# Two self attentions of a perceiver block: turned outputs in the sums' bank, the weighing one step later, projections over four banks

## The reference, cut to what matters

```python
def _L0_attn_ref(x, w_qkv, b_qkv, w_out, b_out):
    qkv = x @ w_qkv + b_qkv
    q, k, v = split into 16 heads of 16          # 4 batches of 256 rows
    attn = softmax(q @ k^T / 4)
    return heads(attn @ v) @ w_out + b_out
def _L1_attn_ref(x, W_qkv, W_proj, b_proj, lambda_q1, ..., subln_w):
    q, k: 32 heads of 8, v: 16 heads of 16       # 4 batches of 256 rows
    o = softmax(q1 @ k1^T) @ v - lam * softmax(q2 @ k2^T) @ v
    o = o * rsqrt(mean(o * o) + EPS) * subln_w * (1 - LAMBDA_INIT)
    return heads(o) @ W_proj + b_proj
```

## Time and profile before

| | us |
|---|---|
| median of 3 executions | 4051.34 (4047.96 to 4053.66) |
| the profiled execution, its own time | 4062.04 |
| its span, first to last instruction | 4059.9 |
| busy in it: PE / DVE / ACT / POOL | 3569.0 / 2493.9 / 2291.5 / 1661.4 |
| first self attention's core | from 1984.1 to 2117.2 |
| second self attention's core | from 3556.5 to 3749.3 |

### The profile page before, as it was taken

The page is one execution under the profiler, slowest core; times in us unless marked ns, Lnnn a source line. Parts: engine busy times, 40 slices in busy tenths (PEclk is TensorE's granted clock), DMA queues, the critical chain, the costliest instruction groups (busy, mean ns, idle before and its releaser), DMA issues. The chain is left out here.

```text
span 4059.9 us, 81431 instructions
## 1 busy us (share of the span) xinstructions
PE 3569.0 (88%) x30262; PEld 2602.5 (64%) x30262; DVE 2493.9 (61%) x3852; ACT 2291.5 (56%) x4294; POOL 1661.4 (41%) x1365
## 2 busy tenths in 40 slices
PE   6899999999999999997777976799999887677399
PEld 4678778777888878885446974455555443333298
DVE  6666666666666666663364113687878777367587
ACT  3666676666766666665242112466666666345165
POOL 1677777777777777767032002101010000024033
PEclk9999999999999999999888987799999999789599
DMA  6677766777767766661303656888878654000011
GB/s 244 250 293 285 273 253 259 278 275 275 260 258 278 272 253 229 246 242 57 86 7 130 256 193 234 184 167 180 168 180 167 128 70 57 15 11 1 21 48 42
DMA packets 231719, 723.30 MB, mean 178 GB/s; under 512 B 47372, under 2 KB 128524, under 8 KB 162444
## 3 DMA queue, kind: packets, MB, share of 16 engines
q1 hardware_dynamic: 228640, 709.70, 55.2%
q0 software_dynamic: 2688, 8.39, 0.6%
HBM read 623.61 MB, written 94.37 MB: 177 GB/s over the span
## 5 line engine op out<-in xcount | busy, mean ns | idle before, releaser
L784 POOL TENSOR_TENSOR wa_acc<-wa_acc,wa_probs 128x512 f32<-128x512 f32 x960 | 1258.2, 1311 | 459.4 <-ACT wa_probs L629 343.2
L694 DVE TENSOR_REDUCE wa_mx<-wa_ps_x 128x1 f32<-128x512 f32 x1024 | 658.6, 685 | 361.2 <-PE wa_ps_x L482 361.2
L629 ACT ACTIVATE wa_probs<-wa_ps_s 128x512 f32<-128x512 f32 x1024 | 531.3, 604 | 547.3 <-PE wa_ps_s L525 546.8
L1326 DVE TENSOR_REDUCE na_mx<-na_ps_m 128x2 f32<-128x1024 f32 x512 | 614.0, 1220 | 208.6 <-PE na_ps_m L1147 204.9
L1271 ACT ACTIVATE na_probs<-na_ps_s 128x512 f32<-128x512 f32 x1024 | 556.5, 595 | 324.1 <-PE na_ps_s L1167 321.7
L621 ACT ACTIVATE wa_ps_s<-wa_m_wide 128x512 f32<-128x512 f32 x1024 | 579.6, 616 | 0.0
L503 PE MATMUL wa_ps_o<-wa_probs,wa_values 128*64 128x256 f32 x4096 | 468.7, 381 | 0.0
L447 PE MATMUL wa_ps_x<-wa_k_ctx,wa_w_k 128*128 128x512 f32 x1488 | 381.0, 403 | 7.4 <-DMA wa_k_ctx<-ctx_split 6.7
L503 PEld LDWEIGHTS wa_ps_o<-wa_probs,wa_values 128*64 128x64 f32 x4096 | 285.4, 137 | 158.4 <-ACT wa_probs L629 23.8
L470 PE MATMUL wa_ps_x<-wa_w_v,wa_v_ctx 128*128 128x256 f32 x2880 | 364.6, 284 | 0.1
L470 PEld LDWEIGHTS wa_ps_x<-wa_w_v,wa_v_ctx 128*128 128x128 f32 x2880 | 357.7, 192 | 6.4 <-issue 0.5
(11 more groups left out here) (347 smaller groups left out, 5735.5 us busy)
## 6 DMA issues: line engine op xcount, KB each, us to landing
wa_k_ctx<-ctx_split SPq DMA_DIRECT2D x248, 1024.0 KB, 7.0
wa_v_ctx<-ctx_split SPq DMA_DIRECT2D x120, 1024.0 KB, 8.2
na_ctx<-ctx_split SPq DMA_DIRECT2D x56, 1024.0 KB, 11.6
na_keys<-k_rows SPq DMA_DIRECT2D x384, 128.0 KB
ctx_split<-wa_stage SPq DMA_DIRECT2D x32, 1024.0 KB, 5.0
w_land<-in_ctxT SPq DMA_DIRECT2D x32, 512.0 KB, 11.1
ge_w_b<-in_w_rows SPq DMA_DIRECT2D x8, 2048.0 KB, 7.8
k_rows<-na_k_high SPq DMA_DIRECT2D x64, 256.0 KB, 3.0
```

Source lines behind the costliest of these rows:

```text
L629: act.activation(probs[:, c % R:c % R + 2, h * SQ:(h + 1) * SQ], ps_s[n % BANKS][:, :].rearrange("p (c n) -> p c n", c=2), ACT.Exp).then_i ...
L694: dve.tensor_reduce(mx[:, half, h, k:k + 1], ps_x[banks[h]][:, :], AX.X, ALU.max).then_inc(m_taken, 1)
L784: pool.tensor_tensor(to[:, :], to[:, :], probs[:, c % R, :], ALU.add).then_inc(summed, 1)
L1326: dve.tensor_reduce(mx[:, half, :, k], ps_m[n % 2][:, :, :], AX.X, ALU.max).then_inc(m_taken, 1)
```

## The change

Four edits, all in self_attention:

1. The turned outputs go into the upper half of ps_o, beside the sums (columns 256 to 511), except those of the last step but one, which stay in ps_q. turn_shift no longer waits for `taken`; weigh does, since it writes the bank that VectorE reads.
2. In TensorE's loop the weighing is that of step n-2 instead of n-1, and stands before scores(n, 0), which itself moves behind turn_shift and maximum.
3. Values and query/key pieces rotate over four banks each instead of two; the values start when their own two DMAs have landed (`wv_in`).
4. VectorE clears ps_o after the first split_maximum instead of before the first maximum; only weigh(0) waits for it.

```diff
+        value_banks = [ps_q, ps_o, ps_m[1][:, 0, :], ps_m[1][:, 1, :]]
+        column_banks = [*ps_s, ps_m[0][:, 0, :], ps_m[0][:, 1, :]]
...
+        def turned(n):
+            return ps_q[:, 0:SQ] if n == STEPS - 2 else ps_o[:, SQ:2 * SQ]
...
-                sp.dma_start(w_sb[:, k, 2 * D:3 * D], w[k * P:(k + 1) * P, 2 * D:3 * D]).then_inc(w_in, 16)
+                sp.dma_start(w_sb[:, k, 2 * D:3 * D], w[k * P:(k + 1) * P, 2 * D:3 * D]).then_inc(wv_in, 16)
...
-                if t >= 2:
-                    pe.wait_ge(v_ready, t - 1)
+                if t >= 4:
+                    pe.wait_ge(v_ready, t - 3)
...
-                if n >= 2:
-                    pe.wait_ge(high_ready, n - 1)
-                    pe.wait_ge(low_ready, n - 1)
+                if n >= 4:
+                    pe.wait_ge(high_ready, n - 3)
+                    pe.wait_ge(low_ready, n - 3)
...
             def turn_shift(n):
                 pe.wait_ge(msplit_ready, n + 1)
-                if n >= 5:
-                    pe.wait_ge(taken, n - 4)
-                elif n:
+                if n:
                     pe.wait_ge(q_ready, n)
...
             def weigh(n):
                 pe.wait_ge(exp_done, 4 * n + 4)
                 if n:
                     pe.wait_ge(ov_ready, n)
+                if 0 < n < STEPS - 1:
+                    pe.wait_ge(taken, n)
+                elif n:
+                    pe.wait_ge(taken, n - 1)
+                else:
+                    pe.wait_ge(zeroed, 1)
...
             def turn_back(n):
                 pe.wait_ge(ov_ready, n + 1)
-                pe.wait_ge(q_ready, min(n + 5, STEPS))
-                if n >= STEPS - 4:
-                    pe.wait_ge(taken, n)
+                if n == STEPS - 2:
+                    pe.wait_ge(q_ready, STEPS)
...
-            pe.wait_ge(w_in, 16 * 2 * KD)
+            pe.wait_ge(wv_in, 16 * KD)
             for t in range(NT):
                 project_values(t)
+            pe.wait_ge(w_in, 16 * KD)
...
-            pe.wait_ge(zeroed, 1)
...
             for n in range(STEPS):
-                scores(n, 0)
+                if n == 0:
+                    scores(n, 0)
                 if n + 2 < STEPS:
                     turn_shift(n + 2)
                 if n + 3 < STEPS:
                     maximum(n + 3, 0)
                     maximum(n + 3, 1)
                 if n >= 2:
+                    weigh(n - 2)
+                if n:
+                    scores(n, 0)
+                if n >= 2:
                     turn_back(n - 2)
                 scores(n, 1)
-                if n:
-                    weigh(n - 1)
+            weigh(STEPS - 2)
             turn_back(STEPS - 2)
...
-            dve.memset(ps_o[:, :], 0.0).then_inc(zeroed, 1)
             for n in range(3):
                 take_maximum(n, 0)
                 if n:
                     shift(n - 1)
                 take_maximum(n, 1)
                 split_maximum(n)
+                if n == 0:
+                    dve.memset(ps_o[:, :], 0.0).then_inc(zeroed, 1)
```

More of the change, by code:

```diff
@@ L1501, in self_attention @@
         ps_q, ps_o = ps_two[1][:, 0, :], ps_two[1][:, 1, :]
-        turned = ps_q[:, 0:SQ].rearrange("p (a i d) -> p a i d", a=2, i=4)
-        w_in, const_in, bias_in = s.sem("w_in"), s.sem("const_in"), s.sem("bias_in")
+        value_banks = [ps_q, ps_o, ps_m[1][:, 0, :], ps_m[1][:, 1, :]]
+        column_banks = [*ps_s, ps_m[0][:, 0, :], ps_m[0][:, 1, :]]
+        wv_in, w_in, const_in, bias_in = s.sem("wv_in"), s.sem("w_in"), s.sem("const_in"), s.sem("bias_in")
         fixed, zeroed = s.sem("fixed"), s.sem("zeroed")
@@ L1580, in project @@
                 th, ct = divmod(n, 4)
-                if n >= 2:
-                    pe.wait_ge(high_ready, n - 1)
-                    pe.wait_ge(low_ready, n - 1)
+                if n >= 4:
+                    pe.wait_ge(high_ready, n - 3)
+                    pe.wait_ge(low_ready, n - 3)
                 for k in range(KD):
-                    ins = pe.matmul(ps_s[n % 2][:, :], w_sb[:, k, ct * P:(ct + 1) * P], xT[:, k, th * 512:(th + 1) * 512],
+                    ins = pe.matmul(column_banks[n % 4], w_sb[:, k, ct * P:(ct + 1) * P], xT[:, k, th * 512:(th + 1) * 512],
                                     start=(k == 0), stop=(k == KD - 1))
@@ L1662, in turn_back @@
                 pe.wait_ge(ov_ready, n + 1)
-                pe.wait_ge(q_ready, min(n + 5, STEPS))
-                if n >= STEPS - 4:
-                    pe.wait_ge(taken, n)
+                if n == STEPS - 2:
+                    pe.wait_ge(q_ready, STEPS)
                 for half in range(2):
-                    ins = pe.transpose(ps_q[:, half * P:(half + 1) * P], ov[n % 2][:, half * P:(half + 1) * P], ident[:, :])
+                    ins = pe.transpose(turned(n)[:, half * P:(half + 1) * P], ov[n % 2][:, half * P:(half + 1) * P], ident[:, :])
                 ins.then_inc(a_done, 1)
-            pe.wait_ge(w_in, 16 * 2 * KD)
+            pe.wait_ge(wv_in, 16 * KD)
             for t in range(NT):
                 project_values(t)
+            pe.wait_ge(w_in, 16 * KD)
             for n in range(8):
@@ L1709, in take_high @@
                 if bias is None:
-                    act.activation(high[:, n, :], ps_s[n % 2][:, :], ACT.Copy).then_inc(high_ready, 1)
+                    act.activation(high[:, n, :], column_banks[n % 4], ACT.Copy).then_inc(high_ready, 1)
                 else:
-                    act.activation(high[:, n, :], ps_s[n % 2][:, :], ACT.Identity, bias=bias_cols[:, n % 4:n % 4 + 1]
+                    act.activation(high[:, n, :], column_banks[n % 4], ACT.Identity, bias=bias_cols[:, n % 4:n % 4 + 1]
                                    ).then_inc(high_ready, 1)
@@ L1756, in take_values @@
                 dve.wait_ge(v_done, t + 1)
-                bank = (ps_o if t % 2 else ps_q)[:, 0:D]
+                bank = value_banks[t % 4][:, 0:D]
                 if diff:
@@ L1809, in take_out @@
             def take_out(n):
+                back = turned(n).rearrange("p (a i d) -> p a i d", a=2, i=4)
                 dve.wait_ge(a_done, n + 1)
@@ L1812, in take_out @@
                     dve.wait_ge(taken, n)
-                link(dve.reciprocal(rden[:, :, :], turned[:, :, :, DV]))
+                link(dve.reciprocal(rden[:, :, :], back[:, :, :, DV]))
                 if not diff:
@@ L1817, in take_out @@
                     for j in range(2):
-                        ins = dve.tensor_tensor(to[:, :, :, (h + j) * DV:(h + j + 1) * DV], turned[:, :, 2 * j:2 * j + 2, 0:DV],
+                        ins = dve.tensor_tensor(to[:, :, :, (h + j) * DV:(h + j + 1) * DV], back[:, :, 2 * j:2 * j + 2, 0:DV],
                                                 rden[:, :, 2 * j:2 * j + 2].unsqueeze(3).to_broadcast([P, 2, 2, DV]), ALU.mult)
@@ L1825, in take_out @@
                     to = o_rows[:, 2 * b:2 * b + 2, 4 * g * DV:4 * (g + 1) * DV].rearrange("p a (i d) -> p a i d", i=4)
-                    dve.tensor_tensor(to, turned[:, :, :, 0:DV], wide, ALU.mult).then_inc(taken, 1)
+                    dve.tensor_tensor(to, back[:, :, :, 0:DV], wide, ALU.mult).then_inc(taken, 1)
                     return
@@ L1830, in take_out @@
                     dve.wait_ge(joined, n // 2 - 1)
-                dve.tensor_tensor(second[n // 2 % 2][:, :, :, :], turned[:, :, :, 0:DV], wide, ALU.mult).then_inc(taken, 1)
+                dve.tensor_tensor(second[n // 2 % 2][:, :, :, :], back[:, :, :, 0:DV], wide, ALU.mult).then_inc(taken, 1)
             dve.wait_ge(fixed, 3)
```

6 lines of the change are left out of this document (3 added, 3 removed).

## The result

4025.9 us (4024.1 to 4028.8) against 4052.3 (4048.0 to 4053.7): ratio 0.9937, 95% interval 0.992 to 0.9955. Both are faster by more than 0.2%, by 26 and 19 us; forecast were 18.

The account below looks back on a forecast made before the run. It took a chain of VectorE work plus one 0.82 us trip to TensorE to bound the first loop. Terms -15.5 - 4.6 - 0.6 - 0.4 + 1.8 + 1.0 = -18.3 gave 4033 us at the median, range 4023 to 4045.

Parts of the forecast that it names:

- loops: Both attention loops: steps of 4.34 in the first and 3.92 in the second, -15.5 us together.
- start: Start of each attention: first value matmul 1.8 us earlier in the first and 2.8 in the second, -4.6 us.
- four banks: Query and key pieces over four banks: a bank wait goes in the first attention, little in the second, -0.6 us.
- clearing: Clearing moved behind the first split: TensorE's first maximum comes earlier, VectorE gives 0.48 back, -0.4 us for both attentions.
- tails: Last steps after the last turn_shift: +0.1 us in the first attention, +1.6 in the second, +1.8 with rounding.
- first steps at the low clock: First full step of each loop at 1.2 GHz: 1.9 and 1.6 us longer, half a chance each, +1.0 net.
- the 3.10: TensorE's run in the loops from one weighing's load to the next, 3.10 us, taken from the last steps before.
- Rival (B): Both loops: TensorE's side is shorter and VectorE binds, steps of 4.18 and 3.87, 4030 us; chance 0.13.
- (C): Both loops: maximum holds the weighing up by 0.91 and 0.65, steps of 4.60 and 4.11, 4041 us; chance 0.16.
- (E): Loops: turn_shift is let go but arrives no earlier because TensorE is still at the second scores, 4048.5 us; chance 0.08.
- (D): Loops: the clock does not come up, each step at 1.2 GHz costs 1.6 to 1.9 us, slower; chance 0.03.
- The added wait: weigh(n-2) waits until VectorE has read output n-3: slack 0.3 us, cost nothing.

Follow-up runs that it names:

- e5: The changed kernel with TensorE's order of before (step n-1 weighed at the end of step n), turned outputs still in the sums' bank: 4159.2 us, ratio 1.027.
- e4: The kernel before with only the first value matmul waiting for just the two value transfers: ratio 0.9985 (0.9975 to 0.9995).
- e2: The changed kernel, unedited, measured and profiled again: 4030.6 against 4050.0 us, ratio 0.995.
- e1: The kernel before, unedited, measured and profiled again: 4050.8 against 4050.0 us, ratio 1.0001.
- e7: The kernel before with the projections over four banks and nothing else: 4053.2 us, one execution.
- e3: The changed kernel with early values, four banks and later clearing undone, so only the two loop edits remain: 4035.1 us, ratio 0.9956.
- e6: The changed kernel with turned outputs back in the shifts' bank and turn_shift waiting for `taken`, later weighing kept: 4047.2 us, ratio 0.9994.
- e12: The changed kernel with the first half of each maximum ahead of turn_shift and its reduction ahead of the shift: 4053.9 us, ratio 1.0009.
- e8: The changed kernel with the second attention's multiplication by minus lambda moved from VectorE to GpSimd: 4027.7 us, one execution.
- e9: The changed kernel with first scores ahead of the weighing, ScalarE's copy between the exponentials and twelve exponential buffers instead of eight: 4032.4 us, one execution.

## Why the prediction was right, and where it was off

Right in direction and range, and in what the change does: turn_shift no longer waits for the outputs, and the new wait on the weighing costs nothing. Wrong in which engine binds afterwards. By the terms of the sum, with both profiles cut as above:

| term | forecast | measured | of it first, second |
|---|---|---|---|
| loops | -15.5 | -21.8 | 10 x 0.53, 13 x 1.27 |
| start | -4.6 | -3.4 | idle -1.9, -2.6; values +1.1, 0 |
| four banks | -0.6 | -0.7 | -0.6, -0.1 |
| clearing | -0.4 | -0.5 | -0.3, -0.2 |
| tails | +1.8 | +1.9 | +0.1, +1.8 |
| first steps at the low clock | +1.0 | +2.3 | +0.8, +1.5 |
| sum | -18.3 | -22.2 | -6.2, -16.0 |

(The columns add up to within 0.1.)

- **The term that was mis-sized: the 3.10 in "0.59 + 0.65 + 3.10 = 4.34 a step" and in "0.36 + 0.44 + 3.10 = 3.90", TensorE's side.** The 0.59, 0.65, 0.36 and 0.44 ahead of it measured 0.63, 0.66, 0.37 and 0.45. But from the weighing's load to turn_shift's load it is 2.88 (2061.94 to 2064.82) and 2.92 (3643.17 to 3646.09), not 3.10; since turn_shift follows VectorE's split there, TensorE's own run is no longer than these. The difference stood in the rows: the 3.10 ends with a weighing's load that stood "[0.25 <-issue]" behind the last scores' load. In the loop turn_shift comes there, and its load follows at once. The same order keeps 3.10 in the last steps after, where a weighing comes again:
```profile
2107.54 0.19 PEld L1646 LDWEIGHTS s_core_ps_two<-s_core_wide,s_core_k_all 128*128 128x128 f32 x1 [0.30 <-ACT s_core_probs L1741]
2107.97 0.56 PEld L1665 LDWEIGHTS s_core_ps_two<-s_core_probs,s_core_v_all 128*17 128x17 f32 x16 [0.24 <-issue]
```
- **Rival (B), VectorE binds, is what came**: 4.18 forecast in the first loop, 4.16 measured, with TensorE level. In the second it gave 3.80 and 3.94 and the steps are 3.65 and 3.83: VectorE's side was 0.1 too long. After an output without lambda the trip to TensorE took 0.54, not 0.60; after one with lambda the next shift starts 3.83 after the last, not 3.94. Its reason, a load pulled past its wait, did not come about: the second scores' load still stands 0.30 for ScalarE. What the prediction drew from the Trainium skill (TensorE: Matmul & The Clock Gate, "Architectural detail: the array is 16× 32×32", on queue depths) therefore gave nearly the right time by the wrong way here.
- **(C)** fell: the weighing's load comes 0.66 and 0.45 after maximum's. **(E)** fell with the loop's steps. **(D)** did not come, but its mechanism is real: e5, where TensorE stands 2 to 3 us a step, ran at 0.66 and 0.59.
- **The added wait** cost nothing, as said: the outputs end 0.83 (2061.11 to 2061.94) and, after an output with lambda, 0.16 (3643.01 to 3643.17) before the weighing's load. The forecast slack was 0.3. e5 shows its price without cover.
- **Start.** Idle time fell by 1.9 and 2.6 for 1.8 and 2.8. That the half clock would last longer into the values was the end of the range, and it took 1.1; in e4 3.4.
- **First steps.** The low clock lasted 27.3 us instead of 20.5, in both attentions and in e2 alike; the steps there are 5.79, and 5.59 and 4.12. I had given each half a chance; both came. In the first attention that goes with the new order: runs with the weighing as before had 20.5 (before, e1, e7) and 23.9 (e4, e5), runs with the later one 27.3 (the change, e2, e3, e6). In the second the old order alone scatters as far, from 20.5 (before, e4) to 30.7 (e1) and 34.1 (e7), so the 1.5 there can't be put down to the change.
- **Tails, right by luck in the first attention.** The 6.7 us taken from the trace before lie partly in a dip of the clock (granted 0.50 from 2105.2 to 2108.6), also in e1 and e7, which neither the changed kernel nor e4 has. From the last shift to the last output it was 13.60 before, 12.39 in e4 (the same order, no dip) and 13.73 after. So the new order costs about 1.3 there, and most of it came back because the clock stayed up.
- Errors of both signs partly cancelled: 6.3 more from the loops, 2.5 less from start and first steps.

## What to carry to other kernels

A wait that is moved to another instruction is only gone if work stands ahead of that instruction: here neither edit was worth anything in the loop alone (e6 0, e5 109 us slower), together they took 21.8 us off the loops, and 16 off the two attentions with tails and first steps (e3). When a run of rows is carried over to a new order, read what each idle piece in it belongs to, its last one above all: it may belong to the successor, which changes. To tell which of two engines a wait follows when both arrive together, compare the lag with that at a place where only one of them was waited for. And cut two profiles at the same instructions before explaining a difference in span.

## What the hardware showed that was not expected

**GpSimd holds up VectorE.** VectorE's first split instruction (L1805 in e12) takes 0.17 us in the loops of the changed kernel. In e12's loops it took 0.70 to 0.99 in every step, once they had settled 0.98 and 0.84:
```profile
2068.67 2.04 POOL L1891 TENSOR_TENSOR s_core_wide<-s_core_q_all,s_core_own_rows 128x512 fp32r<-128x512 f32 x2 [2.55 <-DVE s_core_q_all L1813]
...
2069.76 0.98 DVE L1805 TENSOR_SCALAR s_core_msplit<-s_core_mx 128x8 fp32r<-128x8 f32 x1
...
2070.78 0.17 DVE L1807 SCALAR_TENSOR_TENSOR s_core_msplit<-s_core_mx,s_core_msplit 128x8 fp32r<-128x8 f32 x1
```
It ends at 2070.74, 0.03 after GpSimd's spread (2070.71); in the second loop 3656.86 + 0.84 against 3655.77 + 1.90, again 0.03. The reduction of PSUM beside the same spread kept its 1.22. The Trainium skill (SBUF — State Buffer, "Who interferes with whom") says that a VectorE instruction in a two-port mode and a GpSimd instruction block each other whole; these numbers agree, though no trace shows the mode in which the split runs. In the changed kernel both follow the shift, and two reductions keep the split 0.18 behind the spread's end (2064.20 to 2064.38). e12 takes one of them away from between, and the split runs into the spread. It is not peculiar to e12: at the start of the loops, where only one reduction lies between, the second and third splits of each attention take 0.84 to 1.05 in the kernel before and after alike, and end 0.03 behind the spread. In e8 the added multiplication on GpSimd delays the spread in every other step, and the split is caught by its last 0.04.

**A load behind matmuls of another tile shape.** Behind the last scores' load (128x128) turn_shift's, also 128x128, follows after 0.01 to 0.07. A weighing's (128x17) stands 0.24 to 0.25, in the last steps and in e9, and maximum's (64x128 and 32x128) 0.24 in e12. The shape alone does not do it: behind turn_shift's load (128x128) maximum's follows after 0.06 and 0.07. There the running matmuls have 128 columns, behind the scores 512; which of the two counts, or both, was not tried. The Trainium skill (TensorE: Matmul & The Clock Gate, "The mechanism") says in one place that loads overlap running matmuls only in other row groups, and in another that a load for the background weight buffer goes ahead as well. turn_shift's load at 2064.82 lies beside scores matmuls over the same full rows, whose record (its end is modelled) runs to 2065.11, so the trace does not agree with the first.
